# Down products of a two-layer transformer kernel moved one piece later in the order, with two moved or split helpers

## What is computed

```python
# layer 0
x = res + attention(ada_rms(x)) @ Wo.T            # 8 heads of 64, one key/value head
h = ada_rms(x)                                    # second norm
x = x + silu(h @ Wg.T) * (h @ Wu.T) @ Wd.T        # Wg, Wu: 2048 x 512, Wd: 512 x 2048
# layer 1
h = (x - mu) * rsqrt(var + eps) * (1 + scale) + shift   # third norm
x = x + attention(h) @ Wo.T                       # 16 heads of 32, low-rank keys and values
```

## Time and profile before

| | us |
|---|---|
| median of 3 runs | 895.66 |
| lowest, highest | 894.56, 898.22 |
| the profiled execution, its own time | 898.57 |
| its span, first to last instruction | 896.8 |
| TensorE busy | 856.1 (95%) |
| VectorE busy | 639.8 (71%) |
| ScalarE busy | 448.2 (50%) |
| GpSimd busy | 407.7 (45%) |
| mean granted TensorE clock | 0.987 |

### The profile page before, as it was taken

How to read it: one execution, slowest core, us unless ns; L and a number is a source line. 1 busy time by engine, 2 the same in 40 slices (tenths; PEclk the granted TensorE clock), 3 DMA queues, 4 the chain that set the end, 5 groups by cost and what they waited for, 6 DMA issues and landing times.

```text
span 896.8 us, 15524 instructions
## 1 busy us (share of the span) xinstructions
PE 856.1 (95%) x5864; PEld 707.9 (79%) x5864; DVE 639.8 (71%) x1005; ACT 448.2 (50%) x821; POOL 407.7 (45%) x298
## 2 busy tenths in 40 slices
PE   9898999999999999998898989899999999999997
PEld 6686888888888878876686768788878888878885
DVE  6685667667666667667465877877877877868885
ACT  4665445445445445444435464464554554545652
POOL 2456545545535535446335554444534534532331
PEclk9999999999999999999999999999999999999998
DMA  9801544344433452452332536444354354330001
GB/s 344 334 24 38 169 127 150 112 140 137 133 105 127 124 153 100 120 155 88 138 107 77 187 102 182 135 143 147 123 166 137 117 182 135 112 96 13 25 26 36
DMA packets 114298, 113.54 MB, mean 127 GB/s; under 512 B 57520, under 2 KB 80048, under 8 KB 114224
## 3 DMA queue, kind: packets, MB, share of 16 engines
q1 hardware_dynamic: 113504, 112.45, 39.8%
q10 hardware_dynamic: 720, 0.09, 0.1%
HBM read 88.15 MB, written 24.38 MB: 125 GB/s over the span
## 4 chain that ended last, share of the span: by engine, by line
PE 58%; DVE 13%; ACT 9%; issue 9%; POOL 6%; DMA 4%; SPq 0%; POOLq 0%; ACTq 0%; DVEq 0%
PE ps L640 18%; PE ps L641 17%; PE ps L642 17%; DMA yt<-turned_y 2%; DVE al L1244 2%; ACT yf L1760 2%; POOL gul L511 2%; PE ps L754 1%; DMA turned_y<-ty 1%; ACT ah L1707 1%; ACT L1640 1%; DVE gf L1154 1%; POOL wdl L516 1%; PE ps L915 1%; PE ps L686 1%
## 5 line engine op out<-in xcount | busy, mean ns | idle before, releaser
L511 POOL TENSOR_TENSOR gul<-rgu,guh 128x1024 fp32r<-128x1024 f32 x64 | 156.9, 2452 | 178.4 <-ACT guh L1685 178.4
L1249 DVE TENSOR_TENSOR xres<-ps,xres 128x512 f32<-128x512 f32 x256 | 174.2, 687 | 58.1 <-PE ps L642 58.0
L640 PE MATMUL ps<-h2h,guh 128*128 128x512 f32 x512 | 205.0, 400 | 2.1 <-issue 2.1
L642 PE MATMUL ps<-h2l,guh 128*128 128x512 f32 x512 | 199.9, 390 | 0.0
L641 PE MATMUL ps<-h2h,gul 128*128 128x512 f32 x512 | 199.8, 390 | 0.0
L640 PE MATMUL ps<-wdh,ah 128*128 128x512 f32 x256 | 103.9, 406 | 22.2 <-DVE al L1244 22.1
L640 PEld LDWEIGHTS ps<-h2h,guh 128*128 128x128 f32 x512 | 96.3, 188 | 23.2 <-issue 2.5
L642 PEld LDWEIGHTS ps<-h2l,guh 128*128 128x128 f32 x512 | 96.3, 188 | 21.1
L641 PEld LDWEIGHTS ps<-h2h,gul 128*128 128x128 f32 x512 | 96.5, 188 | 19.5
L641 PE MATMUL ps<-wdh,al 128*128 128x512 f32 x256 | 101.5, 397 | 0.0
L642 PE MATMUL ps<-wdl,ah 128*128 128x512 f32 x256 | 101.5, 396 | 0.0
(11 more groups left out here) (180 smaller groups left out, 1646.2 us busy)
## 6 DMA issues: line engine op xcount, KB each, us to landing
rgu<-gu SPq DMA_DIRECT2D x64, 512.0 KB, 4.0
rwd<-WdT SPq DMA_DIRECT2D x64, 256.0 KB, 3.8
turned_q<-tq SPq DMA_DIRECT2D x20, 320.0 KB, 2.2
qkT<-turned_q SPq DMA_DIRECT2D x20, 320.0 KB, 3.7
turned_p<-tp SPq DMA_DIRECT2D x9, 512.0 KB, 2.6
pT<-turned_p SPq DMA_DIRECT2D x9, 512.0 KB, 3.8
xt<-xT SPq DMA_DIRECT2D x16, 256.0 KB, 2.7
out<-xres SPq DMA_DIRECT2D x15, 256.0 KB, 3.8
```

The costliest lines, as they stand in the source:

```text
L511: pool.tensor_tensor(gul[i][:, :], rgu[i][:, :], guh[i][:, :], ALU.subtract).then_inc(m_gul, 1)
L640: pe.matmul(dst, lh, rh, start=start, stop=False)
L642: return pe.matmul(dst, lh, rl, start=False, stop=stop)
L1249: dve.tensor_tensor(at, bank(BD[i % 2]), at, ALU.add).then_inc(m_x, 1)
```

## The change

The four pieces keep their sizes and fills. Their order from step 2 on changes from

up n, second half of down n-1, gate n+1, first half of down n

to

first half of down n-1, gate n+1, second half of down n-1, up n+1.

On VectorE `low_act(n)` goes to the piece of gate n+1, on ScalarE and GpSimd `high_wd(n)` and `low_wd(n)` go from the piece of gate n to that of the second half of down n-2. `scale_shift_y`, `high_y` and `low_y` go behind the fill before which they stood. The two long subtractions on GpSimd are made in four parts each.

```diff
@@ GpSimd
             def mlp():
                 for n in range(NN):
-                    low_wd(n)
+                    if n < 2:
+                        low_wd(n)
                     yield
-                    if n:
+                    if n > 1:
+                        low_wd(n)
                         yield
...
             def low_w1_queries():
                 pool.wait_ge(w1h, 1)
-                pool.tensor_tensor(w1_cols(wql)[:, :, :, 0:QQ1],
-                                   w1st[:, :].rearrange("p (k c n) -> p k c n", k=KT, c=2),
-                                   w1_cols(wqh)[:, :, :, 0:QQ1], ALU.subtract).then_inc(w1l, 1)
+                for k in range(KT):
+                    ins = pool.tensor_tensor(w1_cols(wql)[:, k, :, 0:QQ1],
+                                             w1st[:, D * k:D * (k + 1)].rearrange("p (c n) -> p c n", c=2),
+                                             w1_cols(wqh)[:, k, :, 0:QQ1], ALU.subtract)
+                ins.then_inc(w1l, 1)
...
-                if s == NT - 1:
-                    low_y(0)
                 if s == NT - 2:
                     low_w1_queries()
                 fill(pieces, f3)
+                if s == NT - 1:
+                    low_y(0)
...
                 fill(pieces, f2 + f3)
+                fill(pieces, f4)
                 if in_layer(u + 2):
                     low_y(u + 2)
-                fill(pieces, f4)
@@ TensorE
                         mm.then_inc(done, 1)
                         yield
-                        if n:
-                            down(n - 1, 2 * w, 2 * w + 2)
+                        if w == 0 and n > 1:
+                            down(n - 2, 2, TPB)
                             yield
+                        if w == 1 and n:
+                            down(n - 1, 0, 2)
+                            yield
+                down(NN - 2, 2, TPB)
+                yield
                 down(NN - 1, 0, 2)
                 yield
@@ VectorE
                 for n in range(NN):
+                    if n:
+                        low_act(n - 1)
                     yield
-                    if n:
-                        add_down(n - 1, 0)
-                        add_down(n - 1, 1)
+                    if n > 1:
+                        add_down(n - 2, 2)
+                        add_down(n - 2, 3)
                         yield
...
                     dve.tensor_tensor(af[:, :], bank(BU), sg[:, :], ALU.mult).then_inc(m_af, 1)
-                    if n == 0:
-                        low_act(n)
                     yield
                     if n:
-                        add_down(n - 1, 2)
-                        low_act(n)
-                        add_down(n - 1, 3)
+                        add_down(n - 1, 0)
+                        add_down(n - 1, 1)
                         yield
+                low_act(NN - 1)
+                add_down(NN - 2, 2)
+                add_down(NN - 2, 3)
+                yield
@@ ScalarE
-                    high_wd(n)
+                    if n < 2:
+                        high_wd(n)
                     yield
-                    if n:
+                    if n > 1:
+                        high_wd(n)
                         yield
...
+                if s == NT - 2:
+                    high_w1_queries()
+                fill(pieces, f3)
                 if s == NT - 1:
                     scale_shift_y(0)
                     high_y(0)
-                if s == NT - 2:
-                    high_w1_queries()
-                fill(pieces, f3)
...
+                fill(pieces, f4)
                 if u < TAIL:
                     scale_shift_y(u + 2)
                     high_y(u + 2)
-                fill(pieces, f4)
```

More of the change, by code:

```diff
@@ L558, in low_w1_queries @@
                 pool.wait_ge(w1h, 1)
-                pool.tensor_tensor(w1_cols(wql)[:, :, :, 0:QQ1],
-                                   w1st[:, :].rearrange("p (k c n) -> p k c n", k=KT, c=2),
-                                   w1_cols(wqh)[:, :, :, 0:QQ1], ALU.subtract).then_inc(w1l, 1)
+                for k in range(KT):
[3 more added lines that the diff above has]
+                ins.then_inc(w1l, 1)
             def low_w1_out():
                 pool.wait_ge(w1h, 4)
-                pool.tensor_tensor(wol[:, :, :], w1st[:, :].rearrange("p (k n) -> p k n", k=KT), woh[:, :, :],
-                                   ALU.subtract).then_inc(w1l, 1)
+                for k in range(KT):
+                    ins = pool.tensor_tensor(wol[:, k, :], w1st[:, D * k:D * (k + 1)], woh[:, k, :], ALU.subtract)
+                ins.then_inc(w1l, 1)
             rstd(0)
```

## The result

The changed kernel takes 918.49 us (median of 4 runs, 917.05 to 919.66), the kernel before 896.15 (4 runs, 894.56 to 898.22) beside it: the ratio is 1.0247, 95% interval 1.0218 to 1.0276. It is slower, as forecast, and 4.6 us above the predicted 913.9. The profiled execution took 917.45 us (span 915.6, granted clock 0.985), which is 18.9 above the 898.57 of the one before; the sum of the terms was 18.2.

The account below looks back on a forecast made before the run. TensorE, 95% busy, was taken to bound the kernel, its waits being what it can gain. Terms 9.1 + 1.4 + 6.0 - 3.3 + 2.3 + 2.7 sum to +18.2 us: 916.8 profiled, 913.9 median; range 901 to 922.

Parts of the forecast that it names:

- Step 1: First fills of eight layer 0 stages (6 to 9, 11 to 14): waits 15.2 us for 6.1, +9.1; bounds 13.8, 17.
- Step 2: First fills of stages 15 and 10: waits of 2.7 for 1.57 and 0.3 for nothing, +1.4 us.
- Step 3: Third fills of stages 6 to 8 and 11 to 13: a new wait of 1.0 each, +6.0 us.
- Step 4: Second fills: VectorE comes 2.3 us after TensorE, enough in both orders, so no change.
- Step 5: Long subtraction at 404.80: the 3.30 us wait for `al` goes whether split or not, -3.3 us.
- Step 6: Turn of the layers: additions late behind scaling, root and second norm, wait 6.6 for 4.28, +2.3 us.
- Step 7: Layer 1: waits of 18.3 us for 15.6, +2.7; least certain term, bounded by -4 and +6.
- Rivals A and B: A: VectorE in time, only the old wait goes, 884.7, chance 0.16; B: waits change places, sum even, about 896, chance 0.08.
- the low bounds: Low ends used for an even sum: first fills +7.7, third fills +3.3, layer 1 -4 us.
- Rival C: TensorE's clock also falls after half of the eight to fourteen new waits, up to +8: 922 us, chance 0.10.
- The rule weighed in the prediction: VectorE's first addition beside GpSimd's sum isn't held, `al` is; were both held, the sum would be some 28 us.

Follow-up runs that it names:

- the run with less of `gul`: Changed kernel with GpSimd's low part of the gate and up weights made on only 64 columns from step 2 on: 917.59 us, ratio 1.0188.
- the cure there: Changed kernel with VectorE's additions first in first and third fills, at the turn and at u = 0 to 2: 893.89 us, ratio 0.9952.
- the kernel with down products around the edges: Changed kernel with another order in each fill: second half of down, gate, up, first half of down: 939.43 us, ratio 1.0455.
- the fastest kernel: Old order, scaling a fill later, split subtractions, first pieces early from stage 6 on, at the turn and u = 0 to 2: 869.29 us, ratio 0.9675.

## Why the prediction was right

The sign, the mechanism and the size held: "the second half wants the banks of the first half emptied by VectorE's additions, just where VectorE is late". 38.1 us of waits that end with `xres` show it, and moving the additions by 1.9 us, alone, removes it. Step by step, in the profiled execution:

- **Step 1, first fills, +9.1.** Seven waits of 1.93 and one of 1.33 (stage 14), 14.9 for 6.1: +8.8. VectorE came 5.12 us after the fill's start where I said 5.27. In stage 14 no square of a first norm stands ahead of the exponential any more (there is no tile left for it), and it starts 0.6 earlier; I had counted that stage with the others. By its own terms the step's upper bound is 17.6, not 17.
- **Step 2, stages 10 and 15, +1.4.** Stage 15: 2.42 and 0.16 for 1.57, in sum 2.6 where I named 2.7, but that is luck, for the reason is one I didn't see: the longest wait is for `gul`, behind the split subtraction on GpSimd. The bank's wait of 2.59 lay beneath it, as the run with less of `gul` showed. Stage 10 was mis-sized: 1.31, not 0.3. Its exponential isn't preceded by a wait for GpSimd's root, so there was no idle time to absorb the later `ah`. Together +2.3.
- **Step 3, third fills, +6.0.** Six waits of 0.93: +5.6.
- **Step 4, second fills, nothing.** No wait there.
- **Step 5, long subtraction, -3.3.** The wait is gone, and it is gone in the run without the split too, so the order did it, as the step said.
- **Step 6, the turn, +2.3.** 6.53 for 4.28. The lower clock was not paid alike in both, as I had it: TensorE was busy at it for 3.4 us before and 5.2 after, some 0.9 us more.
- **Step 7, layer 1, +2.7.** 6.61 at u = 0 (6.5); 1.20 + 2.29 and 1.20 + 2.27 at u = 1 and 2 (3.8 each); 0.42 six times (0.35); and at u = 9 4.35, less the 1.0 of before, where I had 2.1 net. There VectorE also waits 1.22 us for the third norm's root on GpSimd ahead of its softmax, which I had left out. Together 19.4 for 15.6: +3.8.

These sum to 19.5, against 18.9 between the two profiled executions. The forecast for the profiled execution, 916.8, missed by 0.7 us; the median, 918.49, lies 1.0 above that execution, where I had put it 2.9 below (I took the offset of one execution before from its median for the new kernel's). That is 3.9 of the 4.6 us of the miss. Between the medians the change costs 22.3 us, not 18.2: the profiled execution before was slower than the four timed ones, and two of the four after, at 919.5 and 919.7, had a mean clock of 0.981 where the profiled one had 0.985. So the fit to 0.7 us is in part luck: the steps missed by -0.3, +0.9, -0.4 and +1.1, and TensorE happened to be busy for 22.7 us at the lower clock in both profiled executions, in different places.

Two more points, on the rivals and on a part that I didn't price:

- Rivals A and B needed VectorE within 3.3 us, or the low bounds; it came after 5.12. Rival C fell in the profiled execution: after the seven waits of 1.93 and the one of 1.33 the clock stayed at 1.00 (one of them below), and the kernel's mean was 0.985 for 0.987. Its price of 1.2 us for a fall was too low, since the window of the earlier trace rows ended before the stretch did; 1.7 is nearer (last section).
- In step 7 I took the scaling's move for part of the trouble and priced only the whole. That this part alone, in the old order, is worth over 10 us was in the rows I had (4.45, 4.28, 2.92 and 2.09 behind the scaling), and I didn't work it out.

The rule weighed in the prediction was borne out: the addition took 680 ns on average (687 before), while `al`, with both inputs in SBUF, grew to 1438 ns and fell to 785 when GpSimd's subtraction was cut. The Trainium skill (SBUF — State Buffer, Who interferes with whom) says that a VectorE instruction with two inputs in SBUF contends with a GpSimd instruction that reads SBUF, and one with at most one such input doesn't; the trace agrees.

The gain of the scaling's move in the old order is 11 us in the medians. Between the profiled executions of the split alone and of both parts it is 13.8: the waits for `al` (29.1 to 19.9) account for 9.2, and TensorE's busy time at the lower clock (22.9 to 12.6 us, half of it lost) for some 5.

What stays open: the waits of 1.20 at u = 1 and 2 I haven't taken apart; the cure there didn't touch them.

## What to carry to other kernels

When a product's order is changed, list for each fill both what it wants (operands) and what it wants back (banks), and compare each with the moment its maker gets to it: the order that put off `al` pulled forward the additions, and the maker of both was late at the same place. A late engine is cured at its own queue: a few lines that let VectorE do what TensorE waits for before its other work took 15.6 us off the changed kernel and, with the same for ScalarE, 16.6 us off the old order (885.88 to 869.29), while neither of the two new orders of TensorE's pieces gained anything. Taking work away from ahead of the late instruction helps only behind the last wait in that chain (1.1 us taken from ahead of the exponential gave nothing, 1.9 us behind it gave 1.9), and parts of a change should be priced apart, since one can hide the other's gain.

## What the runs showed of the hardware

TensorE's clock after a wait is not decided by the wait's length alone. The windows give start and end, length, busy times of PE, PEld, DVE, ACT and POOL, then the granted clock, DMA share, GB/s. In the changed kernel, behind waits of 2.48, 1.93, 6.53 and 2.29 us, and from 0.66 us after the end of one of 4.35:

```profile
83.90:86.20 2.30, 2.23 (x10) 1.89 (x11) 0.00 (x0) 2.01 (x4) 2.30 (x2) 1.00 0.01 4
...
192.60:193.90 1.30, 1.24 (x6) 1.05 (x6) 1.30 (x3) 1.28 (x2) 0.45 (x1) 1.00 0.52 150
470.18:475.40 5.22, 5.19 (x12) 4.13 (x13) 2.63 (x5) 0.62 (x1) 2.77 (x3) 0.50 0.64 202
...
548.25:550.60 2.35, 2.27 (x10) 1.91 (x11) 2.35 (x2) 2.08 (x3) 2.35 (x2) 1.00 0.91 337
826.90:830.40 3.50, 3.50 (x12) 3.13 (x11) 2.91 (x5) 0.00 (x0) 0.00 (x0) 0.51 0.00 0
```

A clock of 1.00 is the level of 2.4 GHz, 0.50 that of 1.2 GHz. The clearest pair is the wait ahead of the gate product at 84 us: behind its 2.48 us the clock stayed at 1.00 in the changed kernel, and in the run with the order alone it fell 1.3 us after the same wait (2.47) had ended:

```profile
85.20:88.60 3.40, 3.40 (x10) 2.62 (x9) 0.00 (x0) 1.04 (x2) 2.22 (x2) 0.51 0.00 0
```

In the kernel with down products around the edges it was 0.52 behind a wait of 2.38, and 1.00 behind one of 3.46:

```profile
164.10:166.40 2.30, 2.26 (x5) 1.82 (x6) 1.65 (x3) 2.15 (x4) 0.38 (x1) 0.52 0.32 94
...
499.98:502.28 2.30, 2.30 (x11) 2.05 (x12) 2.30 (x5) 0.63 (x1) 0.00 (x0) 1.00 0.99 351
```

What a fall costs: behind the wait of 6.53 twelve matmuls took 5.2 us, where ten run in 2.3 at the upper level, so some 2.5 us; where TensorE was busy for 3.4 us at the lower level, some 1.7. As an estimate, half of TensorE's busy time at the lower level is lost. Added up from windows of a quarter of a microsecond over the whole span, that busy time was 22.7 us in the kernel before, 22.7 in the changed kernel, 22.9 with the split alone, 12.6 with both parts in the old order, 55.6 in the kernel with down products around the edges (mean clock 0.965) and 5.7 in the fastest kernel, where all of it lies in the first 36 us (0.996). So some 8 of the 29 us between the profiled executions before and at 870.02 are the clock, and the rest is waits. Fewer long waits and less time at the lower level went together here, but which wait the clock falls behind varies, and no run isolates what decides it.
